# The norm-and-add stage behind the two picked experts, rewritten with fused VectorE instructions and one GpSimd add

## What is computed

```python
def _layer_norm(x, gamma, beta):
    mu = jnp.mean(x, axis=-1, keepdims=True)
    var = jnp.var(x, axis=-1, keepdims=True)
    return (x - mu) * jax.lax.rsqrt(var + LN_EPS) * gamma + beta
...
    out = _layer_norm(out + x, gamma, beta)
    return out
...
x = x + _L1_ffn_ref(_layernorm(x, axis=-1)[None], ...)[0]
```

## Time and profile before

| | us |
|---|---|
| median of 3 runs | 9338.24 |
| lowest and highest run | 9328.46, 9346.49 |
| the profiled execution's own time | 9342.31 |
| its span in the trace | 9340.6 |
| last VectorE instruction of `ffn1` to the last of `res1b` | 72.53 |
| VectorE busy in that stretch | 49.37 |

### The profile page before, as it was taken

How to read it: one execution, slowest core, us unless ns; L and a number is a source line. 1 busy time by engine, 2 the same in 40 slices (tenths; PEclk the granted TensorE clock), 3 DMA queues, 4 the chain that set the end, 5 groups by cost and what they waited for, 6 DMA issues and landing times. The chain is left out here.

```text
span 9340.6 us, 125383 instructions
## 1 busy us (share of the span) xinstructions
PE 5539.8 (59%) x27247; PEld 4114.1 (44%) x27378; DVE 4119.0 (44%) x10387; ACT 1116.6 (12%) x2497; POOL 3519.1 (38%) x3775
## 2 busy tenths in 40 slices
PE   0805667556996557455634653883788455565556
PEld 0403443334664436333523432772678333454445
DVE  6305544333224337433364331003777555673347
ACT  0200011002331002100210001331000000120011
POOL 1776732770004750377005752002000377007730
PEclk9957778777997768677866766996899677677768
DMA  1503354341002343345002333452110334333420
GB/s 23 225 3 94 104 128 185 104 101 22 13 7 80 104 83 130 113 106 99 11 12 83 105 66 130 149 151 66 49 44 28 96 102 100 83 133 106 106 46 14
DMA packets 344675, 795.08 MB, mean 85 GB/s; under 512 B 117880, under 2 KB 198658, under 8 KB 337026
## 3 DMA queue, kind: packets, MB, share of 16 engines
q0 software_dynamic: 167744, 428.93, 19.0%
q1 hardware_dynamic: 176834, 365.08, 11.2%
HBM read 643.89 MB, written 149.86 MB: 85 GB/s over the span
## 5 line engine op out<-in xcount | busy, mean ns | idle before, releaser
L624 POOL DMA_INDIRECT att_rows_in<-att_table,att_ring_idx x1320 | 1277.2, 968 | 2222.4 <-ACT att_ring_idx L612 1839.5
L701 PE MATMUL ps<-sum_rows_in,sum_hot 128*128 128x256 f32 x3520 | 1327.7, 541 | 1010.2 <-DMA sum_rows_in<-node_table,sum_ring_idx 284.6
L660 DVE TENSOR_TENSOR acc<-acc,ps 128x256 f32 (+2 forms) x1540 | 648.6, 421 | 2159.8 <-PE ps L701 1819.4
L701 PEld LDWEIGHTS ps<-sum_rows_in,sum_hot 128*128 128x128 f32 x3520 | 890.5, 268 | 1348.0 <-issue 1193.3
L624 POOL DMA_INDIRECT sum_rows_in<-node_table,sum_ring_idx x880 | 835.9, 950 | 1411.6 <-ACT sum_ring_idx L612 1160.4
L624 POOL DMA_INDIRECT sum_rows_in<-rel_table,sum_ring_idx x880 | 841.2, 956 | 543.0 <-ACT sum_ring_idx L612 298.0
L701 PE MATMUL ps<-att_rows_in,att_hot 128*128 128x257 f32 x1760 | 653.6, 537 | 501.5 <-DMA att_rows_in<-att_table,att_ring_idx 315.2
L701 PEld LDWEIGHTS ps<-att_rows_in,att_hot 128*128 128x128 f32 x1760 | 449.6, 267 | 704.2 <-issue 619.4
L1415 PE MATMUL ps<-ident,score_ring_e 128*128 128x128 f32 x5280 | 714.0, 279 | 48.6 <-DVE score_top L1266 32.8
L1415 PEld LDWEIGHTS ps<-ident,score_ring_e 128*128 128x128 f32 x5280 | 711.8, 195 | 27.3 <-issue 3.4
L1266 DVE TENSOR_REDUCE score_top<-ps 128x512 f32 (+1 forms) x660 | 429.4, 687 | 167.0 <-PE ps L1415 111.2
(11 more groups left out here) (460 smaller groups left out, 8069.3 us busy)
## 6 DMA issues: line engine op xcount, KB each, us to landing
rel_table<-rel_stage SPq DMA_DIRECT2D x50, 2048.0 KB, 6.3
score_dst_b<-pair_rows SPq DMA_DIRECT2D x132, 640.0 KB, 4.9
ffn_w<-in_L_ffn_W SPq DMA_DIRECT2D x64, 1024.0 KB, 6.9
score_src_b<-pair_rows SPq DMA_DIRECT2D x66, 640.0 KB, 3.9
att_rows_in<-att_table,att_ring_idx POOLq DMA_INDIRECT x1320, 2.8
sum_rows_in<-rel_table,sum_ring_idx POOLq DMA_INDIRECT x880, 2.8
sum_rows_in<-node_table,sum_ring_idx POOLq DMA_INDIRECT x880, 2.8
att_table<-acc SPq DMA_DIRECT2D x15, 650.0 KB, 3.5
```

Of the source, the lines that this page charges most:

```text
L624: pool.indirect_dma_start(rows_in[:, b, u, :], None, table, bass.IndirectOffsetOnAxis(ring_idx[:, b, u:u + 1], 0)).then_inc(gathered[b], 16)
L660: dve.tensor_tensor(K.acc[:, tile, 0:W], K.acc[:, tile, 0:W], K.ps[:, bank, 0:W], ALU.add).then_inc(s_acc, 1)
L701: mm = pe.matmul(K.ps[:, bank, 0:W], hot[:, b, u, :], msg[:, b, u, 0:W], start=i == 0, stop=i == PAIR - 1)
```

## The change

The whole change is in `add_normed`, plus the removal of the second copies of `add_normed` and `top_two_gates` from the file.

- `stats` and `mv` grow from 5 tiles to all 25, and the loop is gone. VectorE makes 25 `bn_stats`, then 25 `bn_aggr`, then one add of the epsilon on 25 columns. None of this waits for a DMA any more.
- It then waits for gamma and beta and runs 25 instructions `aux = (aux - mean) * gamma`, one a tile, 128 x 256 elements, with the mean as a per-partition scalar. Meanwhile ScalarE takes the root of all 25 variances in one instruction.
- Then the reciprocal on 25 columns, a wait for GpSimd, and 25 instructions `x = aux * rstd + x`.
- GpSimd waits for the two DMAs and adds beta to the whole of `x` in one instruction, 128 x 6400 elements. VectorE's wait for it stands ahead of the first of the last 25.
- The phase has 7 semaphores instead of 4. SP issues beta ahead of gamma.

```diff
-        loaded, chain, s_var, s_rstd = (ph.sem(n) for n in ("loaded", "chain", "var", "rstd"))
+        loaded, s_stats, s_mv, s_var, s_rstd = (ph.sem(n) for n in ("loaded", "stats", "mv", "var", "rstd"))
+        s_scaled, s_beta = ph.sem("scaled"), ph.sem("beta")
         gamma, beta = ph.sb("gamma", [P, D]), ph.sb("beta", [P, D])
-        stats, mv = ph.sb("stats", [P, UN, 6]), ph.sb("mv", [P, UN, 2])
+        stats, mv = ph.sb("stats", [P, NT, 6]), ph.sb("mv", [P, NT, 2])
...
+            sp.dma_start(beta[:, :], K.inp[beta_name].partition_broadcast(P)).then_inc(loaded, 16)
             sp.dma_start(gamma[:, :], K.inp[gamma_name].partition_broadcast(P)).then_inc(loaded, 16)
-            sp.dma_start(beta[:, :], K.inp[beta_name].partition_broadcast(P)).then_inc(loaded, 16)
+
+        @block.gpsimd
+        def _(pool):
+            pool.wait_ge(loaded, 32)
+            pool.tensor_tensor(K.x[:, :, :], K.x[:, :, :], beta[:, :].unsqueeze(1).to_broadcast([P, NT, D]), ALU.add).then_inc(s_beta, 1)
 
         @block.scalar
         def _(sc):
-            with sc.Fori(0, NT // UN) as it:
-                hold(sc, s_var, it + 1)
-                sc.sqrt(mv[:, :, 1], mv[:, :, 1]).then_inc(s_rstd, 1)
+            sc.wait_ge(s_var, 1)
+            sc.sqrt(mv[:, :, 1], mv[:, :, 1]).then_inc(s_rstd, 1)
 
         @block.vector
         def _(dve):
+            for t in range(NT):
+                dve.bn_stats(stats[:, t, :], K.aux[:, t, :]).then_inc(s_stats, 1)
+            for t in range(NT):
+                dve.wait_ge(s_stats, t + 1)
+                dve.bn_aggr(mv[:, t, :], stats[:, t, :]).then_inc(s_mv, 1)
+            dve.wait_ge(s_mv, NT)
+            dve.tensor_scalar(mv[:, :, 1], mv[:, :, 1], LN_EPS, None, ALU.add).then_inc(s_var, 1)
             dve.wait_ge(loaded, 32)
-            with dve.Fori(0, NT // UN) as it:
-                turn = LoopChain(dve, chain, it, 2 * UN + 1 + 4)
-                row_stats(turn, dve, stats, mv, [K.aux[:, it * UN + u, :] for u in range(UN)])
-                dve.tensor_scalar(mv[:, :, 1], mv[:, :, 1], LN_EPS, None, ALU.add).then_inc(s_var, 1)
-                hold(dve, s_rstd, it + 1)
-                turn(dve.reciprocal(mv[:, :, 1], mv[:, :, 1]))
-                rows = K.aux[:, bass.ds(it * UN, UN), :]
-                wide = [P, UN, D]
-                turn(dve.tensor_tensor(rows, rows, mv[:, :, 0].unsqueeze(2).to_broadcast(wide), ALU.subtract))
-                turn(dve.tensor_tensor(rows, rows, mv[:, :, 1].unsqueeze(2).to_broadcast(wide), ALU.mult))
-                turn(dve.tensor_tensor(rows, rows, gamma[:, :].unsqueeze(1).to_broadcast(wide), ALU.mult))
-                x_rows = K.x[:, bass.ds(it * UN, UN), :]
-                turn(dve.tensor_tensor(x_rows, x_rows, rows, ALU.add))
-                turn.end()
-            dve.tensor_tensor(K.x[:, :, :], K.x[:, :, :], beta[:, :].unsqueeze(1).to_broadcast([P, NT, D]), ALU.add)
+            for t in range(NT):
+                dve.scalar_tensor_tensor(out=K.aux[:, t, :], in0=K.aux[:, t, :], scalar=mv[:, t, 0:1], in1=gamma[:, :],
+                                         op0=ALU.subtract, op1=ALU.mult).then_inc(s_scaled, 1)
+            dve.wait_ge(s_rstd, 1)
+            dve.reciprocal(mv[:, :, 1], mv[:, :, 1]).then_inc(s_scaled, 1)
+            dve.wait_ge(s_scaled, NT + 1)
+            dve.wait_ge(s_beta, 1)
+            for t in range(NT):
+                dve.scalar_tensor_tensor(out=K.x[:, t, :], in0=K.aux[:, t, :], scalar=mv[:, t, 1:2], in1=K.x[:, t, :],
+                                         op0=ALU.mult, op1=ALU.add)
```

More of the change, by code:

```diff
@@ L2092, in _ @@
             dve.tensor_tensor(K.x[:, :, :], K.x[:, :, :], y, ALU.add)
[L2095 to L2132, removed]
@@ L2135, in top_two_gates @@
-def top_two_gates(K, bias_name, cols):
-    def batch(dve, turn, it, ps, tools):
-        logits, best, marked = (tools.work2[:, :, i * 8:i * 8 + 8] for i in range(3))
-        top = tools.small[:, :, 0]
-        wide = [P, UN, cols]
-        b = tools.vec[bias_name][:, :].unsqueeze(1).to_broadcast(wide)
-        turn(dve.tensor_tensor(logits, ps, b, ALU.add))
-        for u in range(UN):
-            turn(dve.max(best[:, u, :], logits[:, u, :]))
-        turn(dve.tensor_copy(top, best[:, :, 0]))
-        turn(dve.memset(best[:, :, 2:8], BIG))
-        for u in range(UN):
-            turn(dve.match_replace(marked[:, u, :], best[:, u, :], logits[:, u, :], -BIG))
-        dve.tensor_tensor(logits, logits, top.unsqueeze(2).to_broadcast(wide), ALU.subtract).then_inc(tools.s_sum, 1)
-        hold(dve, tools.s_exp, it + 1)
-        turn(dve.scalar_tensor_tensor(out=logits, in0=marked, scalar=-BIG, in1=logits, op0=ALU.is_equal, op1=ALU.mult))
-        turn(dve.tensor_reduce(top, logits, AX, ALU.add))
-        turn(dve.reciprocal(top, top))
-        return dve.tensor_tensor(K.gate[:, bass.ds(it * UN, UN), :], logits, top.unsqueeze(2).to_broadcast(wide), ALU.mult)
-    return batch, 6 + 2 * UN
```

## The result

The changed kernel takes 9368.3 us, median of 11 runs (9343.79 to 9383.44). The kernel before, on the same chips in 11 runs, takes 9342.84 (9324.76 to 9353.88). The ratio is 1.003, with a 95% interval of 1.0019 to 1.004: slower, by some 25 us, where 0.35% faster was forecast. The profiled execution of after is the slowest of its eleven (9383.44 us), so its 41.1 us over the profiled one of before (9342.31) overstate the loss. I read it by phases.

What follows compares the result with a forecast made beforehand. VectorE was taken to bound the 72.53 us phase; start, statistics, add, two passes and reciprocal end at 4751.5 instead of 4784.16, 32.7 us less, net 32.5 after SP's clears. Predicted median 9305.7 us (0.35% less), range 9290 to 9319.

Steps and rivals of the forecast that it cites:

- What bounds the stage: In the changed phase VectorE is the bound, busy 49.37 of 72.53 us; each us leaving its line leaves the program.
- Start, statistics: At the phase's start, bn_stats begins at 4712.7, 4.9 us earlier, without waiting for DMAs; statistics take 10.3 us, to 4723.0.
- the wait at each `bn_aggr`: In the statistics, taken as nothing; 2.1 us if it keeps two bn_aggr from overlapping, hidden under the add.
- The fused passes: Two VectorE passes of 25 scalar_tensor_tensor, 0.40 us a step, 10.1 us a pass; 12.1 without overlap.
- The add: GpSimd's add of beta on 6400 elements takes 13.3 us, from 4717.6 to 4730.9.
- Rivals C and D: GpSimd's add is slow: C, 25 us, total 9317.4, chance 0.09; D, over 45.8 us, kernel slower, chance 0.02.
- case B: The forecast: VectorE's first fused instruction waits for the end of GpSimd's add; net 32.5 us less, 9305.7, chance 0.58.
- Rival A: VectorE and GpSimd run side by side, pass 1 starts at 4723.0; net 40.4 us less, 9297.8, chance 0.27.
- SP's clears: SP clears three more semaphores at the phase's end, 0.06 us each, 0.2 us back.
- The rest of the program: Outside the changed phase the instructions are the same, so only scatter was expected there.
- Rival E: The gain is lost elsewhere, hidden only by scatter; three runs span 18 us, 0.2%; chance 0.04.
- signs of being wrong: Add over 27 us, a fused step over 0.6 us, or something behind the phase moving by over 10 us.

Runs made afterwards that it cites:

- a_chunk5: Changed kernel with one padding semaphore increment and GpSimd's add of beta cut into five instructions of 1280 elements: 9343.7 us, one run, slower chip.
- a_pad67: Changed kernel with 67 more semaphore increments on VectorE behind the epsilon: 9317.67 us, ratio to before 0.9966.
- a_pad1: Changed kernel with one more semaphore increment on VectorE behind the epsilon: 9301.48 us, ratio to before 0.9951.
- b_pad46: Kernel before with 46 semaphore increments on VectorE ahead of its wait for gamma and beta: 9380.2 us, ratio 1.0045.
- b_pad61: Kernel before with 61 semaphore increments on VectorE ahead of its wait for gamma and beta: 9398.89 us, ratio 1.0052.
- b_pad45: Kernel before with 45 semaphore increments on VectorE ahead of its wait for gamma and beta: 9340.3 us, ratio 0.9997.
- a_early: Changed kernel with three padding increments and GpSimd's add of beta moved one phase ahead, into ffn1: 9309.53 us, ratio to before 0.9966.
- a_nobeta: Changed kernel with two padding increments, without GpSimd's add and the wait for it, beta added nowhere: 9304.77 us, one run.
- a_poolpad: Changed kernel with one GpSimd semaphore increment in place of its add, beta added nowhere: 9311.42 us, one run, slower chip.
- a_dve_early: Changed kernel with three padding increments, GpSimd idle, beta added by VectorE at the start of ffn1: 9332.63 us, ratio 0.9965, slower chip.

## Why the prediction was wrong, point by point

- **What bounds the stage**: right. VectorE's line sets its length: 72.53 us became 39.33.
- **Start, statistics**: right within 0.1 us; the wait at each `bn_aggr` cost nothing (1.74 us for 25).
- **The fused passes**: right. 9.97 and 9.99 us against 10.1, so the overlap of 0.08 that I took from `bn_stats` holds for them, and the bound of 12.1 without overlap is out.
- **The add**: 13.66 us against 13.3. The estimate from the Trainium skill ("GPSIMD Engine Reference", section 3.1), 14.1, was as near from the other side. That my 13.3 fits is partly luck: it was the middle between two and three passes of a copy, with no row for either. Rivals C and D, with 25 us and more, are out.
- **Side by side or one after the other**: case B. The rule in "SBUF — State Buffer", section "Who interferes with whom" of the Trainium skill, is borne out, also where it says that a `tensor_scalar` can contend: the epsilon with one input took 8.16 us beside the add and 0.18 without it. I had given that form no part in it, though L897, my only rows for the effect, is just that form. That the two-input form is held too shows in `a_chunk5`, in the three fused instructions of over 3 us. The wrong instruction did no harm, since the epsilon and the first fused one end their wait with the same add. Rival A, with pass 1 from 4723.0, is out: it starts at 4731.05.
- **SP's clears**: 0.88 us to the next issue (4751.27 to 4752.15) against 0.72, so 0.16 against the 0.2 taken.
- **The rest of the program**: here it failed. Rival E reads "The rest of the program has the same instructions, so only scatter can hide it", with a chance of 0.04. The instructions are the same, but 61 places further on in VectorE's program, and so a loop that lay in three fetch blocks lies in four, for 38 us of idle and 50 in the phase. The sum put this term at nothing; it is larger than the whole forecast gain of 32.5 us. The prediction did name this among its signs of being wrong: "if something behind the phase moves by over 10 us".

With the loop back in three blocks the forecast's direction and size stand: -0.34% and -0.49% in `a_pad67` and `a_pad1`, against the -0.35% predicted. That one of them meets it so closely is luck, since the two differ by 16 us and both carry the loss in `sum4` that the sum didn't have.

In the balance of the two profiled executions, `res1b` gives -33.2 and `score2` +50.2; `sum4` adds 5.7 (last section), and the next score phase 12.2; the other 6 us are spread over many phases. The 12.2 show as waits for transfers; VectorE's longest in total in that phase, after and then before:

```profile
DVE score_hit_dst L1354 <- DMA score_dst_b<-pair_rows: 29.3, 18, 1.9
```

```profile
DVE score_hit_dst L1354 <- DMA score_dst_b<-pair_rows: 16.0, 17, 1.9
```

Why these transfers come later isn't shown. On the first chip this phase is within 1.5 us of before in the padded kernels with three blocks, but for +5.2 in `a_pad67`, and +7.2 and +9.8 in `b_pad46` and `b_pad61`; on the slower chip it is +12 to +15 with three blocks. So it scatters, but that the four blocks in `score2` have a part in it isn't excluded.

I could have seen it. Only the list of instructions in order and the length of the loop were needed to see that a 273-instruction loop may lie over three blocks or four. That a fourth costs something, no row of before shows.

## What to carry to other kernels

An edit that changes the number of instructions moves every loop behind it on that engine. After it, compare the packets of the instruction queue, and look for "issue" idle in the loops that were not touched; if it is there, one instruction that does nothing can be worth more than the edit, and a loop of at most 257 instructions (2 x 128 + 1, in three blocks from any place) can't fall into it on an engine like VectorE here. The 257 are worked out from the edge that this one loop of 273 showed; no other length was run. Judge an edit of 0.3% by the length of its own phase and by that of the others apart, not by the total alone. And ask of work moved to GpSimd whether VectorE runs beside it: here the add paid only in a phase where VectorE waits for TensorE, and there it was as well hidden on VectorE itself.

## What the runs showed of the hardware

**Instruction fetch.** VectorE's instructions come in packets of 8 KB, 128 instructions. A loop over three such blocks turns without a fetch. One over four costs five packets and 3.6 to 4.8 us of idle at each turn, and a single instruction decides it: a turn takes 61.9 us in `b_pad45`, 66.9 in `b_pad46` and 68.1 in after. The Trainium skill has the mechanism ("Runtime: NRT & Kernel Launch", section "Instruction fetch mechanics"): a jump back to a target that is no longer in the fetched window waits for a transfer. The traces agree with that. The blocks of 16 KiB that it gives are not what the traces show: the packets are of 8 KB and start one by one. Its 32 KiB do agree, if a block fetched ahead counts.

Why a fourth block doesn't fit, when four of 8 KB make 32 KB, can be read from the start times of packets and instructions (the trace has a record of each of the 273 instructions of a turn). In before's first turn the second and third block are entered at 6603.57 and 6632.88; one packet starts at 6604.51, one at 6633.57, and then none until 7168.16, behind the loop. So the entry into a block fetches the next one, and the loop's three blocks stay beside the one that lies behind it. In after, around the jump back at 6761.01, packets start at 6760.35, 6762.00, 6764.67, 6767.06 and 6797.27. By the same reading the first is the block behind the loop, fetched after the fourth was entered at 6756.79, and the others are the loop's own four, one after the other. A window of four blocks, one of them fetched ahead, gives the five packets a turn and the edge at three. This is an inference from the times, since the records do not name what a packet holds; why the first one starts 3.6 us after the entry, where those of before take 0.9 and 0.7, is open.

**GpSimd's indirect DMAs after a tensor instruction.** In `sum4`, the next phase with much work on GpSimd, its 440 issues of indirect DMAs take 957 ns in the median in all five kernels with an add on GpSimd ahead (after, `a_pad1`, `a_pad67`, `a_early`, `a_chunk5`) and 946 to 947 ns in before and all those without (`a_nobeta`, `a_poolpad`, `a_dve_early`, the shifted kernels of before). The group in `sum4`, of after and then of `a_poolpad` (busy us, mean ns, idle before):

```profile
L624 POOL DMA_INDIRECT sum_rows_in<-node_table,sum_ring_idx x434 | 418.5, 964 | 132.2 <-issue 121.5 <-ACT sum_ring_idx L612 10.1 <-PE ps L701 0.6
```

```profile
L624 POOL DMA_INDIRECT sum_rows_in<-node_table,sum_ring_idx x433 | 413.0, 954 | 131.9 <-issue 123.1 <-ACT sum_ring_idx L612 8.2 <-PE ps L701 0.6
```

440 times 11 ns are 4.8 us, and the phase takes some 581 us against 576 on the first chip. In `a_poolpad` the code of GpSimd is as long as in after, and the median is 946: it is the add that leaves it behind, not the place of the code. In later phases it is gone. So the add on GpSimd costs up to 5 us that the stage doesn't show. On the slower chip the phase differs by less, 581.2 us in `a_chunk5` against 579.0 in `a_poolpad` and 578.0 in `a_dve_early`; VectorE in `ffn1` is still the better place for beta. What the add changes for the DMAs behind it stays open.
